# Attention rows of a Poincaré attention layer: the second exponential as pieces of a VectorE reciprocal

## The reference, cut to what matters

```python
def poincare_fully_connected(x, z, r, c):
    lam = 2.0 / (1.0 - c * jnp.sum(x * x, axis=-1, keepdims=True))
    z_norm = jnp.maximum(jnp.linalg.norm(z, axis=0), EPS)
    two_cr = 2.0 * c_sqrt * r
    inner = x @ (z / z_norm)
    v = 2.0 * z_norm / c_sqrt * jnp.arcsinh(c_sqrt * lam * inner * jnp.cosh(two_cr) - (lam - 1.0) * jnp.sinh(two_cr))
    w = jnp.sinh(c_sqrt * v) / c_sqrt
    return w / (1.0 + jnp.sqrt(1.0 + c * jnp.sum(w * w, axis=-1, keepdims=True)))
...
Q = poincare_fully_connected(x, z_q, b_q, C)
K = poincare_fully_connected(x, z_k, b_k, C)
V = x @ w_v.T + b_v
scores = jnp.einsum('bhqd,bhkd->bhqk', Qh, Kh) / np.sqrt(D_K)
probs = jax.nn.softmax(scores, axis=-1)
out = jnp.einsum('bhqk,bhkd->bhqd', probs, Vh)
```

## Time and profile before

| | |
|---|---|
| median of 3 runs | 2914.53 us |
| lowest, highest | 2914.49, 2916.81 us |
| the profiled execution | 2917.91 us |
| its span, first to last instruction | 2916.1 us |
| mean granted PE clock over the span | 0.981 of 2.4 GHz |
| PE, ACT, DVE, POOL busy over the span | 2685.2, 2041.1, 1869.6, 1195.4 us |
| stage b, first to last probability tile | 1352.3 to 2540.3 us |

### The profile page before, as it was taken

The page is one execution under the profiler, slowest core; times in us unless marked ns, Lnnn a source line. Parts: engine busy times, 40 slices in busy tenths (PEclk is TensorE's granted clock), DMA queues, the critical chain, the costliest instruction groups (busy, mean ns, idle before and its releaser), DMA issues. The chain is left out here.

```text
span 2916.1 us, 53192 instructions
## 1 busy us (share of the span) xinstructions
PE 2685.2 (92%) x20501; PEld 1216.8 (42%) x20501; DVE 1869.6 (64%) x2438; ACT 2041.1 (70%) x2691; POOL 1195.4 (41%) x735
## 2 busy tenths in 40 slices
PE   2899999999999999976999999999999999999997
PEld 1456556555555444332333333333333333344443
DVE  8999999999996445576455555555555451335544
ACT  6554554555434555557999898999999999855554
POOL 4889999999994122010404141413131210022200
PEclk8899999999999999988999999999999999999999
DMA  2010010100003122116565655555655556222102
GB/s 87 1 33 26 29 41 24 36 29 31 12 29 122 44 72 72 58 58 116 72 126 91 130 91 125 91 125 88 139 88 123 90 105 140 42 87 81 58 20 73
DMA packets 167241, 211.73 MB, mean 73 GB/s; under 512 B 16968, under 2 KB 118904, under 8 KB 167032
## 3 DMA queue, kind: packets, MB, share of 16 engines
q1 hardware_dynamic: 167032, 208.83, 31.4%
HBM read 149.97 MB, written 58.81 MB: 72 GB/s over the span
## 5 line engine op out<-in xcount | busy, mean ns | idle before, releaser
L2067 ACT ACTIVATE b_pr<-b_ps 128x1024 f32<-128x1024 f32 x1024 | 994.5, 1034 | 85.0 <-PE b_ps L2142 79.0
L2142 PE MATMUL b_ps<-b_st 128*32 128x512 bf16 x8192 | 614.6, 382 | 46.7 <-ACT b_pr L2067 29.1
L2210 PE MATMUL b_acc<-b_pr,b_vaug 128*32 128x512 f32 x4096 | 530.1, 592 | 5.3 <-DVE b_osb L1901 3.2
L2142 PEld LDWEIGHTS b_ps<-b_st 128*32 128x32 bf16 x8192 | 177.4, 95 | 593.9 <-ACT b_pr L2067 383.5
L1353 PE MATMUL f_po<-f_s,o_weights 128*128 128x512 f32 x768 | 351.9, 601 | 10.0 <-DVE o_res L1135 6.3
L1123 DVE TENSOR_TENSOR f_turned<-f_cs,f_s 128x1024 f32<-128x1024 f32 x96 | 119.3, 1243 | 355.5 <-ACT f_cs L1256 350.1
L749 PE MATMUL a_pv<-a_xnT,o_big 128*128 128x512 f32 x512 | 249.2, 610 | 54.2 <-DVE a_mem L498 45.0
L1216 ACT ACTIVATE f_h<-f_po,o_weights 128x512 f32<-128x512 f32 x192 | 131.9, 687 | 213.9 <-PE f_po L1353 213.9
L741 PE MATMUL a_pu<-a_xnT,o_big 128*128 128x512 f32 x512 | 236.6, 606 | 28.9 <-DVE o_weights L450 23.0
L1722 POOL TENSOR_TENSOR b_SQ<-o_big 128x1024 f32<-128x1024 f32 x28 | 58.3, 2082 | 478.9 <-DVE o_big L1824 478.9
L1353 PEld LDWEIGHTS f_po<-f_s,o_weights 128*128 128x128 f32 x768 | 140.5, 190 | 213.1 <-issue 158.5
(11 more groups left out here) (291 smaller groups left out, 4447.1 us busy)
## 6 DMA issues: line engine op xcount, KB each, us to landing
b_st<-b_scratch SPq DMA_DIRECT2D x512, 128.0 KB, 6.5
o_res<-x SPq DMA_DIRECT2D x30, 1024.0 KB, 7.0
b_scratch<-b_parts SPq DMA_DIRECT2D x32, 768.0 KB, 4.7
o_big<-x SPq DMA_DIRECT2D x17, 1024.0 KB, 8.1
x<-o_res SPq DMA_DIRECT2D x15, 1024.0 KB, 4.5
o_res<-in_L_attn_a_x_dram SPq DMA_DIRECT2D x18, 512.0 KB, 4.5
x<-o_res SPq DMA_DIRECT2D x32, 256.0 KB, 2.2
o_res<-in_L_attn_a_x_dram SPq DMA_DIRECT2D x28, 256.0 KB, 2.7
```

The source lines that it names most:

```text
L2067: nc.scalar.activation(pr[:, 4 * (blk % 2) + j, :], ps[:, j % 2, :], ACT.Exp, scale=SC).then_inc(S["probs_done"], 1)
L2142: x = nc.tensor.matmul(o[r:r + 32], w[:, r:r + 32], v, start=start, stop=stop, skip_group_check=True)
L2210: x = nc.tensor.matmul(acc[32 * j:32 * j + 32, h * 512:(h + 1) * 512], vaug[:, kt, c:c + 32], pr[:, 4 * (kt % 2) + j, h * 512:(h + 1) * 51 ...
```

## The change

In the steady batches the step `down` leaves ACT. In its place DVE computes the reciprocal of `EP` into `SQ`, in 4 pieces of 256 columns for each tile: 16 new steps `inv`, spread over blocks 6, 7, 10, 11 and 15 to 18. `inv` 0 of a tile waits for `up`; `inv` 3 of a tile counts the new semaphore `inv_done`, and the subtraction on POOL, which keeps the step's name `down`, waits for that. Some steps move to make room: the POOL subtraction of tiles 0 and 2 one block later, `stats` one block earlier (10 to 9), `ln` 3 and `up` 3 one block earlier, `sign` 2 one block later. The set-up keeps the exponential.

```diff
-    6: [("square", 2, 1, 0), ("down", 0, 1, 2), ("proja", 7, 1, 0), ("projb", 7, 1, 2)],
-    7: [("ln", 1, 1, 0), ("out", 6, -1, 0), ("out", 7, -1, 2)],
+    6: [("square", 2, 1, 0), ("inv", 0, 1, 0), ("proja", 7, 1, 0), ("projb", 7, 1, 2), ("inv", 1, 1, 0)],
+    7: [("ln", 1, 1, 0), ("inv", 2, 1, 0), ("inv", 3, 1, 0), ("down", 0, 1, 0), ("out", 6, -1, 0), ("out", 7, -1, 2)],
...
-    15: [("down", 2, 1, 0), ("v", 7, 1, 0)], 16: [("ln", 3, 1, 0), ("sum", 0, 1, 0), ("sign", 2, 1, 0)], 17: [("up", 3, 1, 0), ("fac", 0, 1, 0)],
-    18: [("down", 3, 1, 0), ("row", 0, 1, 0), ("out", 2, 0, 2)], 19: [("sign", 3, 1, 0), ("out", 3, 0, 2)],
+    15: [("ln", 3, 1, 0), ("inv", 8, 1, 0), ("v", 7, 1, 0), ("inv", 9, 1, 0)],
+    16: [("up", 3, 1, 0), ("inv", 10, 1, 0), ("sum", 0, 1, 0), ("inv", 11, 1, 0), ("down", 2, 1, 0)],
+    17: [("fac", 0, 1, 0), ("sign", 2, 1, 0), ("inv", 12, 1, 0), ("inv", 13, 1, 0)],
+    18: [("row", 0, 1, 0), ("inv", 14, 1, 0), ("inv", 15, 1, 0), ("down", 3, 1, 0), ("out", 2, 0, 2)], 19: [("sign", 3, 1, 0), ("out", 3, 0, 2)],
...
-ACT_KINDS = ("square", "root", "ln", "up", "down")
+ACT_KINDS = ("square", "root", "ln", "up")
...
                     if kind == "down":
-                        pool.wait_ge(S["e_done"], 8 * b + 2 * i + 2)
+                        pool.wait_ge(inv_done, 4 * (b - 1) + i + 1)
...
+                    if kind == "inv":
+
+                        q, c = i // 4, slice(i % 4 * 256, (i % 4 + 1) * 256)
+                        if i % 4 == 0:
+                            dve.wait_ge(S["e_done"], 8 * b + 2 * q + 2)
+                        x = nc.vector.reciprocal(SQ[:, q, c], EP[:, q % 2, c])
+                        if i % 4 == 3:
+                            x.then_inc(inv_done, 1)
```

More of the change, by code:

```diff
@@ L1447 @@
     5: [("root", 1, 1, 0), ("up", 0, 1, 2), ("proja", 6, 1, 0), ("y", 1, 1, 0), ("projb", 6, 1, 2)],
-    6: [("square", 2, 1, 0), ("down", 0, 1, 2), ("proja", 7, 1, 0), ("projb", 7, 1, 2)],
-    7: [("ln", 1, 1, 0), ("out", 6, -1, 0), ("out", 7, -1, 2)],
+    6: [("square", 2, 1, 0), ("inv", 0, 1, 0), ("proja", 7, 1, 0), ("projb", 7, 1, 2), ("inv", 1, 1, 0)],
+    7: [("ln", 1, 1, 0), ("inv", 2, 1, 0), ("inv", 3, 1, 0), ("down", 0, 1, 0), ("out", 6, -1, 0), ("out", 7, -1, 2)],
     8: [("root", 2, 1, 0), ("sign", 0, 1, 0), ("v", 0, 1, 0), ("y", 2, 1, 0)],
-    9: [("up", 1, 1, 0), ("v", 1, 1, 0)],
-    10: [("square", 3, 1, 0), ("v", 2, 1, 0), ("stats", 0, 2, 0)],
-    11: [("down", 1, 1, 0), ("v", 3, 1, 0), ("rstd", 0, 2, 0)],
+    9: [("up", 1, 1, 0), ("v", 1, 1, 0), ("stats", 0, 2, 0)],
+    10: [("square", 3, 1, 0), ("inv", 4, 1, 0), ("v", 2, 1, 0), ("inv", 5, 1, 0)],
+    11: [("inv", 6, 1, 0), ("v", 3, 1, 0), ("inv", 7, 1, 0), ("down", 1, 1, 0), ("rstd", 0, 2, 0)],
     12: [("ln", 2, 1, 0), ("v", 4, 1, 0), ("sign", 1, 1, 0)],
@@ L1559, in phase_b @@
         st_loaded = [s.sem(f"st_loaded{i}") for i in range(2)]
+        inv_done = s.sem("inv_done")
         row_stored, row_loaded = s.sem("row_stored"), s.sem("row_loaded")
@@ L2051, in step @@
                             act.wait_ge(S["d_done"], n - 1)
-                        nc.scalar.activation(EP[:, i % 2, :], SQ[:, i, :], ACT.Exp, scale=zn2[:, i:i + 1]).then_inc(S["e_done"], 1)
+                        nc.scalar.activation(EP[:, i % 2, :], SQ[:, i, :], ACT.Exp, scale=zn2[:, i:i + 1]).then_inc(S["e_done"], 2 if b else 1)
                     if kind == "down":
```

## The result

The changed kernel takes 2985.79 us, median of 4 runs (2978.55 to 2988.60), against 2914.51 for the kernel before (4 runs). The ratio is 1.0238 with a 95% interval of 1.0226 to 1.0250: 71 us slower. The profiled execution has a span of 2984.1 us. Lines of stage b have moved by 3 to 11: L2067 is now L2078, L2142 L2153, L1901 L1912, L1824 L1827.

A forecast was written before the change was run, and what follows sets the result against it. ACT was taken to bound only blocks with a step. Place 1, place 2 and the clock, 0.6 + 10.7 + 1.2 = 12.5 us a batch, times 7 = 87 us on 2917.9, gave a forecast of 3000 us, range 2955 to 3035.

The forecast's parts named there:

- What bounds the kernel: ACT bounds blocks with a step, by some 0.7 us each; PE, in order, waits for DVE and POOL at fixed places.
- place 2: Blocks 16 to 20, first `take_acc` to `sum` 1: chain grows from 18.1 to 28.8 us, 10.7 more.
- The price of a piece: One reciprocal of 256 columns on DVE: 2.1 us, bounds 1.75 to 2.3.
- Place 1: Blocks 6 to 9, three pieces before the outs and `take_acc`: PE 2.4 us later, 0.6 left at block 16.
- the 0.8 for `down` 1: ACT time given back beside the values `v`, counted as PE catching up between blocks 10 and 15: 0.8 us a batch.
- The clock and the restart: After PE idles 7 us at block 20, 3 to 5 us at half pace cost 1 to 2 us; 1.2 taken.
- The sum: Whole batch: 0.6 + 10.7 + 1.2 = 12.5 us more, times 7 = 87 us.
- What lies behind the sum keeps its distance: Late steps behind `sum` 1 (factors of K through HBM, `scale`, `split`) add nothing; blocks 21 to 31 stay as long.
- Hidden on DVE: Rival: DVE absorbs pieces of 0.45 us, chain 19.2 us, batch gains 1 to 2.6 us: 2896 to 2907; 7 in 100.
- no change: Rival: a piece of 0.6 to 0.9 us leaves the time as it was; 3 in 100.
- the case of 1.75 us and no clock loss: Rival: PE loses little at block 20, 7.7 us a batch, 54 in all: 2968 us; 25 in 100 for this lower half.
- The forecast case: Pieces of 2.0 to 2.3 us with a short loss of clock: 2985 to 3020 us; 52 in 100.

The follow-up runs named there:

- e1: The changed kernel with each of the 112 reciprocals on 16 of its 256 columns, order and waits unchanged: 2904.41 us, ratio 0.9962 to the kernel before.
- e9: e7 with `out` 6, 7 before `inv` 2, 3, `sign` 0 later, `sum` 1, `fac` 1 in block 22, `row` 1, `split` 0 in 23, `row` 0 after head 2: 2900.50 us.
- e8: The kernel before with only `sum` 1, `fac` 1, `row` 1 and `scale` 2 later (blocks 22, 23, 24, 25): 2930.36 us, ratio 1.0051.
- e10: The changed kernel with one reciprocal of 1024 columns per tile, at the place of its last piece: 3019.88 us, ratio 1.0351 to the kernel before.
- e5: The changed kernel with POOL's root ahead of its subtraction of tile 2 and `sign` 2 behind `inv` 12 and 13: 2979.20 us, ratio 1.0210 to the kernel before.
- e7: e5 with `sum` 1 moved to block 22, `fac` 1 to 23, `row` 1 to 24, `scale` 2 to 25: 2924.18 us, ratio 1.0029 to the kernel before.

## Why the prediction was right, point by point

Predicted were 3000 us (2955 to 3035), measured 2985.79. The mechanism was right, two waits of PE in its written order at the end of chains through DVE and POOL; the sizes of three terms were off, and in part cancel.

- **What bounds the kernel.** Right. ACT gives back 0.7 us in each of blocks 16 and 17 and 0.6 in block 6, where 1.3 and 0.5 were worked out; PE meets DVE and POOL at the two places named, and one more on the way (`row` 0, named as part of place 2).
- **The price of a piece.** This is the term that was sized wrong: 2.1 us predicted, 1.73 measured, at the low end of the bounds. The runs give 0.231, 1.730 and 6.551 us for 16, 256 and 1024 columns, so (1.730 - 0.231)/240 = 6.25 and (6.551 - 1.730)/768 = 6.28 ns a column. The raw slope of the two rows, 6.5, was nearly right, but by luck: the two differ by 52 ns, and in e1 the reciprocals of 16 columns from SBUF alone scatter from 193 to 255 ns (their mean of 231 is only 28 ns above that of 8 columns). My correction for PSUM, taken from a scalar operation, made it 7.9 and was wrong. The estimate of 8.3 ns from the Trainium skill ("VectorE: DVE Perf Modes", repeat count of 8) is not borne out here: 6.25 ns is 6 cycles of the 0.96 GHz that page gives.
- **Place 1.** Predicted 2.4 us of delay at `take_acc` and 0.6 left at block 16. In the timed batch `take_acc` is 1.9 late against the start of its block, and the sum of the differences of blocks 6 to 15 is +1.2. The delay is smaller with the cheaper piece, but less comes back than I thought: blocks 10 to 13 lose 0.45 instead of gaining 0.8 and more. Blocks 10 and 11 together gain 0.3 with pieces of 0.23 us (9.63 instead of 9.96 in e1) and 0.6 in e9, so the 0.8 for `down` 1 was an overestimate. Blocks 10 to 15 together came out even (+0.01), where 1.8 us of catching up were worked out. In 3 of the 7 profiled batches the clock is at half at the end of block 9, which adds to it: without that block 9 takes 5.75 us where the batch has `out` 6 and 7, with it 6.19 to 6.65.
- **Place 2.** Predicted 28.8 us, measured 25.3; before 18.1. The six pieces take 9.9 us in it where the sum had 12.4, which is 2.5 of the 3.5. Another 0.5 is the last link: I counted 0.6 us from the end of `pair` 1 to the sum, as in before, and it was 0.06. In before PE did not wait there, so these 0.6 us were the reserve of a chain that I said had none. Every link stands in the timeline in the order of the working, the late root (`fac` 0 at 1767.73 with 3.55 us of idle DVE) included.
- **The clock and the restart.** Predicted 1.2 us. From `sum` 1 to the first exponential of block 21 it is 1789.18 - 1784.67 = 4.5 us in the timed batch and 4.3 in the mean, before 1760.04 - 1757.54 = 2.5, and block 21 is 0.3 longer in the mean: 2.1 us. The two rows of before, then those of the changed kernel (the last exponential of block 20 and the first of block 21, at 1789.18):

```profile
1756.03 3.77 ACT L2067 ACTIVATE b_pr<-b_ps 128x1024 f32<-128x1024 f32 x4 [0.27 <-PE b_ps L2142]
1760.04 1.94 ACT L2067 ACTIVATE b_pr<-b_ps 128x1024 f32<-128x1024 f32 x2 [0.24 <-PE b_ps L2142]
```
```profile
1786.62 1.02 ACT L2078 ACTIVATE b_pr<-b_ps 128x1024 f32<-128x1024 f32 x1 [6.71 <-PE b_ps L2153]
1789.18 1.94 ACT L2078 ACTIVATE b_pr<-b_ps 128x1024 f32<-128x1024 f32 x2 [1.54 <-PE b_ps L2153]
```

  The 2.1 us hold the half clock (the sum itself takes 1.04 instead of 0.69) and also something I left out: after the wait the two score tiles are empty, and ACT has nothing until PE has written one.
- **The sum.** Predicted 0.6 + 10.7 + 1.2 = 12.5 us a batch; measured 1.2 + 7.0 + 2.1 = 10.3 (7.0 is the 7.2 by which the chain is longer, less 0.2 by which its `take_acc` comes earlier in block 16, 0.91 instead of 1.15). The direction, the places and their order of size are right. How near the total came is in part luck: place 2 was put 3.7 us too high, place 1 and the restart 1.5 us too low, and the two partly cancel.
- **What lies behind the sum keeps its distance.** Right for the changed kernel (blocks 22 to 31 are the same to 0.01 us; block 21, which was to stay too, is 0.3 longer). It holds only as long as `row` 1 keeps its distance to `scale` 2, as e8 showed.
- **The rivals.** "Hidden on DVE" falls with the price: no piece costs 0.45 us. Its own working does not hold together. By the sum, 28.8 - 6 x 1.6 = 19.2 us is still 1.1 longer than 18.1, and the chain breaks even at some 0.3 us a piece (28.8 - 18.1 = 10.7, 1.8 less for each of six) and not at 0.8. e1 has pieces of 0.23 us, a chain of 17.3 us and a gain of 8 us; it bears out the sum, but no run has a piece of 0.45 us or of 0.6 to 0.9, so neither the 7 to 18 us of this rival nor the condition of "no change" was tested. Of the slower ones the case of 1.75 us and no clock loss gave 2968; the price was that case's, the loss of clock was not absent. The forecast case itself asked for pieces of 2.0 to 2.3 us, and the measured 1.73 is also just under the lowest mean named as a sign (1.75). So 2985.79 lies in the interval of the forecast case, at its lower end, without the price on which that case rested.

## What to carry to other kernels

Before work is moved to an engine that is idle half the time, follow the chain of single steps that ends at an in-order wait of the bounding engine: each microsecond put into that chain beyond its reserve is paid in full (3.1 us more in e10 cost 3.2, 1.8 less in e5 gave back 1.6), and idle time elsewhere on the engine does not help. If the chain has room behind it, move the wait and not the work: here a sum two blocks later, the root ahead of the subtraction, and outputs ahead of the pieces instead of behind them, turned 71 us of loss into a gain of 14. And when a shared table is moved, look for the next in-order wait behind it (`scale` 2 behind the transfer, `inT` behind `scale` 2).

## What the runs showed of the hardware

- VectorE's reciprocal in float32 takes 6.25 to 6.28 ns a column from 16 to 1024 columns (means 0.231, 1.730, 6.551 us), five times a two-tensor operation (1.23 us for 1024), with SBUF source and target. A reciprocal beside a running POOL operation was not held: the three pieces at 1710.96 take 4.97 us, with a POOL square at 1711.13 that itself took its usual 1.89.
- A scalar operation on 8 columns took 2.04 us instead of 0.17 while POOL's subtraction ran (e5). The Trainium skill ("SBUF — State Buffer", on the shared port pair) says that of a GpSimd operation and a VectorE operation that needs the pair the second to start is held until the first has ended; the trace agrees for the scalar operation, which ends 0.03 us after the subtraction (1762.55 and 1762.52).
- After PE's wait of 5.9 us in block 20 the granted clock was 0.50, the level of 1.2 GHz, for 6.8 us in the timed batch and for 6.8 to 10.2 in all 7. After the waits of 1.6 us in block 9, which 6 of the batches have, it fell in 3 only (for 3.4 us; with the same waits in all 6 in e5 and in none in e7), so equal batches differ by up to 0.9 us there (block 9: 5.74 to 6.65).
